# Third layer of a four-layer model: the short convolution done by TensorE, state rows issued by ScalarE, nine weight buffers and another order of work

## The reference, cut to what matters

```python
xz = x @ W_in
xc, z = jnp.split(xz, 2, axis=-1)
xc_t = lax.conv_general_dilated(xc_t, conv_w, padding=[(D_CONV - 1, 0)], feature_group_count=D_INNER, ...)  # 4 taps, one filter per channel
xc = silu(xc + conv_b)
x_dbl = xc @ W_x                      # one column for dt, 16 for B, 16 for C
dt = softplus(dt_raw @ W_dt + b_dt)
def step(h, inp):                     # over the tokens
    dA = exp(dt_t[..., None] * A)
    h = dA * h + dt_t[..., None] * B_t[:, None, :] * x_t[..., None]
    y = einsum('bds,bs->bd', h, C_t)
```

## Time and profile before

| | us |
|---|---|
| median of three runs | 1758.94 |
| the profiled execution | 1759.55 |
| its span (first to last instruction) | 1757.6 |
| TensorE busy in the span | 1571.4 |
| VectorE busy in the span | 1246.5 |
| ScalarE busy in the span | 1154.2 |
| the third layer, about | 1199 to 1615 |

### The profile page before, as it was taken

The page is one execution under the profiler, slowest core; times in us unless marked ns, Lnnn a source line. Parts: engine busy times, 40 slices in busy tenths (PEclk is TensorE's granted clock), DMA queues, the critical chain, the costliest instruction groups (busy, mean ns, idle before and its releaser), DMA issues. The chain is left out here.

```text
span 1757.6 us, 19878 instructions
## 1 busy us (share of the span) xinstructions
PE 1571.4 (89%) x6998; PEld 682.6 (39%) x7006; DVE 1246.5 (71%) x1752; ACT 1154.2 (66%) x1608; POOL 234.7 (13%) x230
## 2 busy tenths in 40 slices
PE   6999999999999999997999899999656677668998
PEld 3333333333333333332444466663224344333675
DVE  5977777777777777761343338776897889966997
ACT  5788888888888888885524387335636645523773
POOL 1001111111111011121000100000580000284000
PEclk9999999999999999999999899998887788877999
DMA  6200101010000000001142121113344656531000
GB/s 209 45 13 1 31 7 25 13 25 12 25 12 21 16 1 13 7 1 58 36 90 70 26 63 50 39 37 89 128 135 146 199 166 196 183 108 38 1 1 25
DMA packets 66571, 103.64 MB, mean 59 GB/s; under 512 B 8999, under 2 KB 32518, under 8 KB 66452
## 3 DMA queue, kind: packets, MB, share of 16 engines
q1 hardware_dynamic: 64426, 98.18, 19.4%
q0 software_dynamic: 2048, 4.20, 0.8%
HBM read 86.39 MB, written 15.87 MB: 58 GB/s over the span
## 5 line engine op out<-in xcount | busy, mean ns | idle before, releaser
L708 DVE TENSOR_REDUCE best<-quad 128x2 f32<-128x1024 f32 x256 | 309.9, 1222 | 130.3 <-PE quad L498 127.9
L622 ACT ACTIVATE weights<-quad 128x1024 f32<-128x1024 f32 x256 | 255.7, 1029 | 28.6 <-PE quad L523 28.3
L2617 PE MATMUL quad<-l_st,ident 128*128 128x512 f32 x256 | 144.8, 713 | 52.7 <-DVE l_st L2932 52.7
L540 PE MATMUL quad<-weights,values 128*32 128x512 f32 x1024 | 136.4, 605 | 0.4 <-ACT weights L622 0.4
L110 PE MATMUL quad<-q,wf 128*128 128x512 f32 x256 | 121.5, 606 | 0.7 <-DVE mk L679 0.3
L110 PE MATMUL quad<-hid,wf 128*128 128x512 f32 x256 | 116.6, 599 | 0.0
L2915 DVE TENSOR_TENSOR l_st<-l_u,l_bs 128x1024 f32<-128x1024 f32 x64 | 76.7, 1219 | 42.9 <-PE quad L2617 29.0
L2617 PEld LDWEIGHTS quad<-l_st,ident 128*128 128x128 f32 x256 | 56.2, 233 | 120.4 <-DVE l_st L2932 63.4
L566 ACT ACTIVATE hid<-quad,col 128x512 f32<-128x512 f32 x128 | 84.9, 688 | 21.4 <-PE quad L110 21.3
L110 PE MATMUL quad<-sq_all,mean_w 128*128 128x512 f32 x176 | 94.5, 636 | 1.9 <-ACT sq_all L1367 0.9
L498 PE MATMUL quad<-ks,qs 48*128 48x512 bf16 x512 | 89.5, 385 | 6.8 <-DVE best L708 6.3
(11 more groups left out here) (448 smaller groups left out, 3033.3 us busy)
## 6 DMA issues: line engine op xcount, KB each, us to landing
l_bs<-xd_dram SPq DMA_DIRECT2D x32, 512.0 KB
l_c_rows<-xd_dram SPq DMA_DIRECT2D x32, 512.0 KB
l_weights<-in_F_w SPq DMA_DIRECT2D x45, 257.0 KB, 3.4
end_cs<-comb SPq DMA_DIRECT2D x32, 256.0 KB, 3.7
l_cs<-comb SPq DMA_DIRECT2D x32, 256.0 KB, 3.6
wf<-in_L_f SPq DMA_DIRECT2D x16, 256.0 KB, 2.6
qs<-q_dram SPq DMA_DIRECT2D x16, 192.0 KB, 3.4
ks<-k_dram SPq DMA_DIRECT2D x16, 192.0 KB, 4.3
```

The costliest lines, as they stand in the source:

```text
L540: last = nc.tensor.matmul(out[32 * j:32 * j + 32, :], values[:, kt, GH * g + j, :], weights[p % BUFS][:, j % 2, j // 2, :], start=(kt == 0 ...
L622: nc.scalar.activation(weights[p % BUFS][:, slot, :, :].rearrange("p a t -> p (a t)"), doubles.of("weigh", m, i), ACT.Exp, scale=scale).th ...
L708: nc.vector.tensor_reduce(heads[:, :, slot, qt, c], doubles.of("search", m, i).rearrange("p (a t) -> p a t", a=2), AX.X, ALU.max).then_inc ...
L2617: last = nc.tensor.matmul(y[d][:, c:c + BANK], core.ident[:, :], st[n % RING][:, c:c + BANK], start=False, stop=(s == NS - 1), skip_group_ ...
```

## The change

- **Convolution.** `convolve`, `copy_x`, `xpad` and their semaphores go. POOL multiplies `w_in` by the four taps (`taps`, 128x1024, from a new host array `A2_conv` spread over the partitions by one more DMA of 512 KB, L2491). PE's `convolved` makes each bank of x by four products of 512 columns (the later banks of a half) or 512, 511, 510 and 509 columns (the first), one for each tap, added up in PSUM. `silus` reads that bank with the convolution's bias: eight activations of 128x512 for four of 128x1024. `dt` has its own buffers.
- **Rows of B and C** are issued by ACT (L2847) in place of SP, with the same waits.
- **Weights** have nine buffers in place of six; the last three are parts of `rows`, the scatter's source, so block 6 waits until the scatter is done. `outs` shares its place with `taps`.
- **Order.** Every row of `PLAN_2` has new numbers.

The numbers of `PLAN_2` say little; here is one line of it, and the rest of the diff, cut to its core:

```diff
-    "x": (8, 9, 11, 14, 15, 16, 17, 18,),
+    "x": (9, 11, 12, 13, 26, 29, 30, 39,),
...
-    RING, KEPT_WEIGHTS = 4, 6
+    RING, KEPT_WEIGHTS, OWN_WEIGHTS = 4, 9, 6
...
+        outs_all = sb("outs", [P, 2, 4, D])
+        outs = [outs_all[:, i, :, :] for i in range(2)]
+        taps = outs_all[:, :, :, :].rearrange("p i k d -> p (i k d)").rearrange("p (k e) -> p k e", k=CONV)
...
+        conv_rows = bs[0]
...
+        weights = [kept[:, i * W:(i + 1) * W] for i in range(OWN_WEIGHTS)] + [rows_flat[:, i * W:(i + 1) * W] for i in range(KEPT_WEIGHTS - OWN_WEIGHTS)]
...
+                        if b == OWN_WEIGHTS:
+                            sp.wait_ge(scattered, 16 * 2 * TILES)
                         if b >= KEPT_WEIGHTS:
                             sp.wait_ge(made, (b - KEPT_WEIGHTS) // 4 + 1)
...
                 ahead.load(sp)
+                sp.dma_start(conv_rows[:, :], a["A2_conv"].partition_broadcast(P)).then_inc(conv_rows_landed, 16)
...
             def _(pool):
+                pool.wait_ge(in_landed, 16)
+                pool.wait_ge(conv_rows_landed, 16)
+                nc.gpsimd.tensor_tensor(taps[:, :, :], conv_rows[:, :].rearrange("p (k e) -> p k e", k=CONV),
+                                        w_in[:, 0:DD * P].rearrange("p (k e) -> p k e", k=1).to_broadcast([P, CONV, DD * P]), ALU.mult).then_inc(taps_done, 1)
                 link(nc.gpsimd.memset(w_dt[:, :], 0.0))
...
+                def convolved(h):
+                    for i in range(DD):
+                        for c in range(2):
+                            yield at("x", 4 * h + 2 * i + c)
+                            pe.wait_ge(taps_done, 1)
+                            pe.wait_ge(normalised, 2 * h + c + 1)
+                            ring_free(pe, "x", 4 * h + 2 * i + c)
+                            to = ring.of("x", 4 * h + 2 * i + c)
+                            first = h * T + c * BANK
+                            for k in reversed(range(CONV)):
+                                back = CONV - 1 - k
+                                missing = 0 if c else back
+                                last = nc.tensor.matmul(to[:, missing:BANK], taps[:, k, i * P:(i + 1) * P], core.xn[:, first - back + missing:first - back + BANK],
+                                                        start=(k == CONV - 1), stop=(k == 0), skip_group_check=True)
+                            last.then_inc(x_ready[h], 1)
...
-                def copy_x(h):
+                def silus(h):
...
+                            nc.scalar.activation(xc[h][i][:, c * BANK:(c + 1) * BANK], ring.of("x", 4 * h + 2 * i + c), ACT.Silu, bias=cols[:, i, CB:CB + 1]
+                                                 ).then_inc(silu_done[h], 1)
...
-                        sp.dma_start(tiles[k % 2][:, :], xd_dram[h, first + s].partition_broadcast(P)).then_inc(landed[k % 2], 16)
+                        act.dma_start(tiles[k % 2][:, :], xd_dram[h, first + s].partition_broadcast(P)).then_inc(landed[k % 2], 16)
...
-                def convolve(h):
-                    for d in range(DD):
-                        yield at("conv", 2 * h + d)
-                        x = xpad[h][d]
-                        dve.wait_ge(x_copied[h], 2 * d + 2)
-                        nc.vector.tensor_scalar(xc[h][d][:, :], x[:, 0:T], cols[:, d, 0:1], cols[:, d, CB:CB + 1], ALU.mult, ALU.add).then_inc(conv_done[h], 1)
-                        for k in range(1, CONV):
-                            dve.wait_ge(conv_done[h], CONV * d + k)
-                            nc.vector.scalar_tensor_tensor(out=xc[h][d][:, :], in0=x[:, k:k + T], scalar=cols[:, d, k:k + 1],
-                                                           in1=xc[h][d][:, :], op0=ALU.mult, op1=ALU.add).then_inc(conv_done[h], 1)
```

More of the change, by code:

```diff
@@ L2186 @@
 PLAN_2 = {
-    "var": (4, 5, 6, 12,),
-    "x": (8, 9, 11, 14, 15, 16, 17, 18,),
-    "z": (13, 20, 21, 23, 42, 44, 47, 49,),
-    "xd": (22, 24, 31, 32,),
-    "dt": (25, 26, 28, 29, 36, 37, 38, 52,),
-    "out": (105, 106, 163, 164,),
-    "logits": (19,),
-    "ranks": (30,),
-    "turn": (40,),
-    "rows": (10, 27, 33, 35,),
-    "turned": (56, 57, 65, 66, 83, 84, 99, 110, 114, 116, 129, 132,),
-    "hidden": (60, 61, 62, 69, 74, 78, 79, 82, 90, 92, 96, 100, 107, 108, 113, 118, 123, 125, 130, 131, 137, 139, 140,),
@@ L2206 @@
-    "slots": (24, 27, 28, 29, 32, 37, 55, 59, 66, 75, 89, 101,),
-    "store": (42, 48, 78, 79, 87, 97, 102, 113, 114, 123, 126, 127,),
-    "comb": (88, 131,),
+    "var": (5, 6, 7, 8,),
+    "x": (9, 11, 12, 13, 26, 29, 30, 39,),
+    "z": (14, 35, 36, 94, 37, 49, 53, 54,),
+    "xd": (15, 16, 41, 42,),
+    "dt": (17, 19, 20, 21, 47, 48, 50, 52,),
+    "out": (151, 152, 163, 164,),
+    "logits": (10,),
+    "ranks": (18,),
+    "turn": (22,),
+    "rows": (23, 24, 25, 27,),
+    "turned": (62, 63, 72, 73, 82, 86, 96, 102, 108, 113, 119, 124,),
@@ new lines @@
+    "gate_z": (14, 53, 55, 147, 54, 74, 75, 79,),
+    "copy_xd": (16, 17, 66, 67,),
+    "lin": (18, 19, 24, 25, 68, 69, 76, 77,),
+    "abs": (20, 26, 83, 87,),
+    "exp": (21, 27, 88, 90,),
+    "ln": (23, 28, 89, 97,),
+    "exp_a": (9,),
+    "decay": (32, 33, 35, 41, 43, 44, 48, 49, 51, 57, 59, 62, 70, 71, 72, 73, 80, 86, 91, 92, 93, 96, 102, 103, 110, 111, 112, 120, 128, 129, 130,
+        138, 142, 144, 145, 150, 151, 156, 160, 167, 168, 172, 173, 182, 183, 192, 195, 198, 199, 202, 203, 206, 207, 212, 217, 221, 225, 226, 236,
+        244, 247, 248, 249, 263,),
```

186 lines of the change are left out of this document (85 added, 101 removed).

## The result

| | before | after |
|---|---|---|
| median (range) | 1760.04 us (1758.12 to 1763.32) | 1713.05 us (1712.55 to 1715.47) |
| ratio, 95 % interval | | 0.9734 [0.9716, 0.9752] |
| profiled execution, its span | 1759.55, 1757.6 | 1713.21, 1711.5 |
| third layer begins (TensorE's first centring) | 1199.5 | 1202.2 |
| first scan | 1256.6 | 1250.9 |

47 us faster, where 32 were forecast (1727 us, from 1758.94). The whole difference lies in the third layer, and most of it between the first scan and the gates: 348.8 us before, 306.0 now. The layer itself began 2.7 us later. The work ahead of it is the same in both kernels, and over all runs this point scatters by more (see the end), so the start is best read from there: 57.1 us to the first scan before, 48.7 now.

What follows compares the result with a forecast made beforehand. VectorE was taken as the bound: a gain of 65.3 us less the new order's waits W, seven terms summing to 33.5, left 31.8 us, so 1727 us. The range was 1709 to 1750.

Steps and rivals of the forecast that it cites:

- rival 4: The order is as good as it reads: nothing late, gathers balanced, W 15.5, gain 50, 1709 us; chance 0.12.
- W: Waits the new order has between first scan and gates, taken off the 65.3 us gain: forecast 33.5, before 53.6.
- The start: Third layer up to the first scan: convolution off VectorE brings the first scan to 1247.1, 9.5 us earlier.
- first slots: Term (a): waiting for the first slots, which the scatter fills; 9.6 us before becomes 0 to 9.6, taken as 1.
- rows late: Term (b): VectorE's waits for rows of B and C, now issued by ScalarE; 10.0 us before, taken as 3.
- gathers: Term (c): waits from the 32 gathers late in the layer, their plan just balanced; taken as 6 us, bounds 0 and 14.4.
- other lag of adds: Term (d): VectorE's waits for adds apart from slots and gathers; 11.7 us before, taken as 12.
- weights: Part of term (d): waits for expert weights left with nine buffers, 3 us; bounds with the 12 are 5 and 25.
- ScalarE's waits: Term (e): ScalarE has 102 us of work in turns of 107; taken as 6 us, bounds 3 and 20.
- rival 1: The waits stay, rows and weights sharing transfer engines as before: W 53.6, gain 11.7, 1747 us; chance 0.15.
- Rival 2: Transfers become the bound in the experts' stretch, 258 GB/s needed: gain 9, 1750 us; chance 0.11.
- Rival 3: TensorE's clock stays low through the 64 turns, at 1.2 GHz making the kernel slower: 1783 us; chance 0.07.

Runs made afterwards that it cites:

- rows_sp: The changed kernel with the rows of B and C issued by SP again; 1715.37 us, ratio to before 0.9747.
- taps_first: The changed kernel with the taps' row as the layer's first transfer, ahead of w_in; 1716.30 us, ratio to before 0.9762.
- nine: The kernel before with nine weight buffers in place of six, nothing else changed; 1747.94 us, ratio to before 0.9903.
- conv_dve: The changed kernel with the whole convolution on VectorE again, order of everything else kept; 1735.91 us, ratio to before 0.9857.
- eight: The changed kernel with eight weight buffers in place of nine, order unchanged; 1728.99 us, ratio to before 0.9825.
- split_late: split with some of ScalarE's scale steps set behind decays and the first two expert sums set later; 1715.83 us, ratio to before 0.9751.
- late: The changed kernel with split_late's move of scale steps and sums alone; 1725.64 us, ratio to before 0.9807.
- split: The changed kernel with one of four convolutions on VectorE, logits ahead of the third bank of x, z later; 1710.83 us, ratio to before 0.9718.
- after again: The changed kernel itself, run again on another chip; 1715.11 us, ratio to before 0.9759.

## Why the prediction was right, and where it was off

The direction and the bound held, and of the mechanism most did; the reason given for the rows and the weights (ScalarE's issue) did not. The size fell short by 14 us, 1727 for 1713.05, near the low end of the range and near rival 4 (1709), which the text gave 0.12.

- *VectorE is the bound, and its work can be added up.* Right. The gates could have started 289.9 + 3.1 us behind the first scan; they did so after 306.0, so the new waits are W = 13.0 us, where before they were 53.6. One reading in the account of these 53.6 is off: the 1.7 us for the first decay are idle time ahead of the first scan, which itself starts at 1256.6, so 4.1 and not 2.4 are longer instructions.
- *The start, 9.5 us earlier.* Close: 8.4 us, counted from the layer's start. The taps' 1.5 us of waiting, inside the bound of 0 to 5, did not move the start of x. What moved the first scan were the twelve x products behind the logits, 12.2 us and not 10.3, part of them at the lower clock: in rows_sp and taps_first, with 10.5, the first scan stands 46.9 us behind the layer's start.
- *W = 33.5.* **This sum failed**, by 20.5 us. Its terms against the pauses above:

| term | forecast | after |
|---|---|---|
| first slots | 1 | 5.2 |
| rows late | 3 | 0 |
| gathers | 6 | 2.2 |
| other lag of adds | 12 | 0.7 |
| weights | 3 | 4.8 |
| ScalarE's waits | 6 | 0 (the decay that was late is the gathers' 2.2) |
| longer instructions | 2.5 | 2.2 |
| last gates' wait, held at 3.1 outside of W | 0 | 1.0, so -2.1 |

The term that failed most is (d), "other lag of adds": the 11.7 us of before were carried over as if they belonged to TensorE's work, with a little more for the denser order. Counting all adds but those behind the first slots and the gathers, weights included, the traces have 11.7 us before, 9.5 with nine buffers in the old order, 17.2 with the new order and eight, and 5.5 with the new order and nine, where 15 were forecast (12 and 3 for weights). So it went with order and buffers together and not with the buffers alone; the order alone was not run. ScalarE's term was built rightly: 20 table loads were counted and 20 came, and its 102 us compare with 84.4 us of work and 24 row issues of 0.33, 92 in 111 us. It does not follow that a busy engine is waited for; the order had the decays far enough ahead. Where a sum of seven small waits is taken each at a cautious value, the total lies far above the likeliest one: only two of the seven, slots and weights, came out above, by 6.0 us together; the other five came out 24.4 below, and the gates' wait 2.1.
- *Rows late, from ScalarE's issue: the reason was wrong.* The wait for rows did go, yet with SP issuing them it went as well (rows_sp), and in the old order ScalarE's issue made it worse (23.2 us for 10.0). Most of it went with the buffers: in nine, with the old order and SP's issue, 2.2 of the 10.0 us are left, and SP's wait for a free buffer is 0.2 us where it was 41.1. That SP's waiting in front of a row is an in-order queue being blocked is true as read, and cost nothing that can be told: SP stood 158.9 us in front of rows in rows_sp. The prediction named the 101.7 us of waiting in front of rows of B as one cause of late weights; the runs point to the other one that it names, the wait for a buffer that an earlier block holds. By the rule that was weighed against ScalarE's issue (the Trainium skill, DMA: Bandwidth & Descriptors, Issuing engines are not separate DMA queues), another issuing engine saves only the sequencer's time. The runs agree with it: 0.9747 [0.9702, 0.9792] with SP, 0.9759 [0.9708, 0.9810] with ScalarE. What the prediction drew from the rule, that the experts' waits would then stay (rival 1), does not follow, since the buffers take part of them out (28.8 to 16.4 us in nine) and the whole change leaves 9.2.
- *Rival 2, transfers.* 238 GB/s at a share of 0.76 in the experts' stretch, near the 258 forecast as demand; not a bound. *Rival 3, clock.* The granted clock rose from 0.85 to 0.91 in the same window, as argued.
- *From the gates on nothing changes.* Within 2.5 us: from the gates to the start of the last layer it took 1.4 us longer, and the last layer 1.1. The first of these has a cause that the prediction did not look at, GpSimd's joins of the experts (last section). Together: 31.8 forecast + 20.5 (W) - 1.1 (start) - 2.7 (layer began later) - 2.5 (behind the gates) = 46.0, the difference of the spans being 46.1.
- *What the signs said.* Gates at 1556.8 and not 1573; last gather at 1541.8 and not 1530; ScalarE busy 0.76 and not over 0.9; weights 9.2. The last gather is a miss in the other direction: the gathers ended 12 us later than forecast and did little harm, the 2.2 us of one late decay, since only `scale` and the sums need them.

How the gain of 47 us divides, as far as it can: nine buffers in the old order have 14 us of it. The changed kernel with the convolution still on VectorE has 24 (conv_dve), and is 21 us slower than the changed kernel. These 21 are not all the convolution's: 9.4 and 3.3 are its work and the start, and 7.1 are waits in an order that was made without it, in an execution with slow gathers. The parts hang together, so they do not add up to 47 in one way only. The new order gives more with nine buffers than with eight (12 to 16 us); what it gives with the old six was not run. The change's issue of rows gives nothing that can be told.

## What to carry to other kernels

A long wait in an issuing queue is no loss by itself: ask what is behind it, and whether its buffer would be free any sooner. Where an order has been balanced, one buffer less (eight) or work put back (conv_dve) is paid for elsewhere as well. A step that waits for a slow chain, here a scale for a gather, holds up what stands behind it on its engine, so put it behind the work that the bound needs, and look which banks the steps between will want (split_late, late). Before a late step is put down to the order, compare the lengths of what it waited for (split). And do not carry a leftover wait over into a new order without its cause; say of each what it is made of, or it becomes the largest error of the sum.

## What was not expected of the hardware

- 32 indirect gathers took 71.2 us from the first start to the end of the last in after, and 61.4 in the kernel before, with the same work; single ones take 0.94 to 4.3 us in these two. Over all traces it was 60.8 to 62.2 us in the four kernels with the old order, and 69.1 to 80.5 in the ten with the new one; in split and conv_dve, the two longest, three single ones took 6.42 us. Why was not tested.
- Products of 512 columns against the taps took 0.51 us a record (24 in 12.23) beside the 0.43 read elsewhere, and 0.44 (24 in 10.54) in taps_first. The mean granted clock of that stretch was 0.86 in the one and 1.00 in the other, so some records went at the 1.2 GHz level in one execution and none in the other, with the same products ahead of them. after again, late and eight have 12.23 as well, rows_sp has 10.54.
- The start of the third layer differs between executions of programs that are the same up to there: 1197.5 to 1205.0 us. Points of time inside the layer should be counted from its start.
- The border behind the layer has two ends to wait for. From VectorE's last join to the last layer's first product 1.5 to 5.7 us go by. In eight of the fourteen traces that product starts 6.75 to 6.79 us behind the end of GpSimd's last join of the experts, and in the other six 1.46 to 1.51 us behind VectorE's last join, whichever is later. The four kernels with the old order are of the second kind, the changed kernel is of the first:

```profile
1561.21 1.26 POOL L2551 TENSOR_TENSOR x<-x,l_slots 128x512 f32<-128x512 f32 x1
1569.19 0.54 POOL L3168 MEMSET l_raw<- 32x128 f32 x2 [6.72 <-POOLq L88]
```

  So when it ran again and its gates started 2.6 us later, the last layer still began at 1569.2. What fills these 6.7 us the traces do not say. Its joins wait for VectorE's joins of the first half (10.9 us in after), so they are a place to look next; no run tried it.
